# Token-major down and output projections, a new order in head and tail, and the mask of the maxima on DVE

## The reference

```python
xn = layernorm(x)                                   # over the 256 features, no weights
q, k, v = xn @ Wq.T, xn @ Wk.T, xn @ Wv.T           # 16 heads of 16
att = q @ k.T / 4 + causal_mask                     # 512 x 512 for each head
s = (softmax(att) @ v) @ Wo.T
g = silu( down( silu(gate(xn)) * up(xn) ) )         # 704 hidden; integer weights minus 128, times a scale per output row
out = x + s * g
```

## Time and profile before

| | us |
|---|---|
| median of 3 runs | 343.92 (342.92 to 345.23) |
| the profiled execution | 342.69 |
| its span | 340.7 |
| PE, DVE, ACT, POOL busy in the span | 304.8, 215.6, 168.8, 112.4 |

### The profile page before, as it was taken

How to read it: one execution, slowest core, us unless ns; L and a number is a source line. 1 busy time by engine, 2 the same in 40 slices (tenths; PEclk the granted TensorE clock), 3 DMA queues, 4 the chain that set the end, 5 groups by cost and what they waited for, 6 DMA issues and landing times.

```text
span 340.7 us, 5720 instructions
## 1 busy us (share of the span) xinstructions
PE 304.8 (89%) x2192; PEld 197.6 (58%) x2192; DVE 215.6 (63%) x364; ACT 168.8 (50%) x238; POOL 112.4 (33%) x179
## 2 busy tenths in 40 slices
PE   0695779999999989999999989999999999998855
PEld 0573447666565546766655547767656566664323
DVE  5799755644579986454769986554765666447113
ACT  3544325634475647343375646443475665336720
POOL 4014434311364552100355462100346662012310
PEclk9997879999999999999999999999999999999987
DMA  7846772078840003296750010187680100001201
GB/s 281 241 155 172 191 116 62 9 180 169 197 75 0 4 9 117 68 191 175 162 92 2 1 64 0 52 187 182 156 111 0 36 32 4 0 4 62 65 0 62
DMA packets 21150, 31.40 MB, mean 92 GB/s; under 512 B 2420, under 2 KB 10100, under 8 KB 21124
## 3 DMA queue, kind: packets, MB, share of 16 engines
q1 hardware_dynamic: 20672, 30.37, 37.5%
q10 hardware_dynamic: 452, 0.67, 0.6%
HBM read 20.19 MB, written 10.49 MB: 90 GB/s over the span
## 4 chain that ended last, share of the span: by engine, by line
PE 68%; DVE 19%; DMA 4%; ACT 4%; issue 3%; SPq 1%; POOL 0%; POOLq 0%; DVEq 0%; ACTq 0%
PE ps L349 14%; PE ps L351 12%; PE ps L350 11%; PE ps L518 10%; PE ps L499 7%; PE ps L458 6%; PE ps L470 4%; DVE mx L934 3%; DVE mx L932 3%; ACT hid L662 2%; DVE xn L900 2%; PE ps L526 2%; DVE hid L919 2%; DMA qk_scratch<-xr 2%; DVE nw L893 1%
## 5 line engine op out<-in xcount | busy, mean ns | idle before, releaser
L725 ACT ACTIVATE pt<-ps 128x1024 f32<-128x1024 f32 x80 | 81.8, 1023 | 24.5 <-PE ps L499 24.4
L839 POOL TENSOR_SCALAR_AFFINE_SELECT pt<-pt 128x256 f32<-128x256 f32 (+1 forms) x112 | 48.1, 442 | 128.7 <-ACT pt L725 128.7
L932 DVE TENSOR_REDUCE mx<-ps 128x2 f32<-128x1024 f32 x32 | 38.9, 1221 | 11.8 <-PE ps L470 11.1
L458 PE MATMUL ps<-kp,qp 48*128 48x512 f32 (+3 forms) x256 | 37.0, 347 | 9.3 <-DMA kp<-qk_scratch 3.5
L825 POOL TENSOR_TENSOR hl<-hid,hh 128x512 fp32r<-128x512 f32 x24 | 31.2, 1301 | 42.3 <-ACT hh L676 41.9
L819 POOL TENSOR_TENSOR hid<-hid 128x512 f32<-128x512 f32 x24 | 30.7, 1278 | 42.5 <-ACT hid L669 42.3
L518 PE MATMUL ps<-pt,vt 128*17 128x256 f32 (+3 forms) x512 | 43.8, 437 | 0.8 <-POOL pt L839 0.8
L349 PE MATMUL ps<-xh,guh 128*128 128x512 f32 x96 | 43.3, 451 | 0.0
L499 PE MATMUL ps<-qp,kp 50*128 50x512 f32 (+3 forms) x256 | 40.1, 370 | 2.9 <-DVE mx L935 1.6
L351 PE MATMUL ps<-xh,gul 128*128 128x512 f32 x96 | 38.7, 403 | 0.0
L350 PE MATMUL ps<-xl,guh 128*128 128x512 f32 x96 | 38.6, 402 | 0.0
(11 more groups left out here) (104 smaller groups left out, 495.1 us busy)
## 6 DMA issues: line engine op xcount, KB each, us to landing
qk_scratch<-hid SPq DMA_DIRECT2D x24, 256.0 KB
qp<-qk_scratch SPq DMA_DIRECT2D x14, 256.0 KB, 4.8
kp<-qk_scratch SPq DMA_DIRECT2D x14, 256.0 KB, 6.8
qp<-qk_scratch SPq DMA_DIRECT2D x18, 128.0 KB, 5.2
kp<-qk_scratch SPq DMA_DIRECT2D x18, 128.0 KB, 7.1
xr<-in_x SPq DMA_DIRECT2D x4, 512.0 KB, 4.1
out<-xr SPq DMA_DIRECT2D x8, 256.0 KB, 2.3
xin<-in_x SPq DMA_DIRECT2D x3, 512.0 KB, 3.7
```

Source lines behind the costliest of these rows:

```text
L458: nc.tensor.matmul(ps[:, base + e, c:c + w], qp[part, place(b, half), col, i * P:(i + 1) * P], kp[part, place(b, half), col, 0:w], start=( ...
L725: nc.scalar.activation(pt[:, 2 * kk:2 * kk + 2, :], ps[:, base:base + 2, :], ACT.Exp, scale=SCALE).then_inc(exp_done, 1)
L839: mm = nc.gpsimd.affine_select(out=diag, in_=diag, compare_op=ALU.is_ge, fill=0.0, base=0, pattern=[[0, diag.shape[1]], [1, P]], channel_m ...
L932: mm = nc.vector.tensor_reduce(mg[:, :, kk, 3], both, AX.X, ALU.max, negate=True)
```

## The change

- The causal mask of the maxima is added by DVE, to the diagonal blocks in PSUM, in all pairs from the ninth on (72 of 80); the first eight keep their mask matmuls. DVE waits for its own add before the reduction. POOL makes the mask tile `tri`.
- `down` and the output projection have the tokens on the partitions: stationary is the activation (128 x 128), moving the weight with 256 columns. "dn" and "o" have twice as many matmuls of half the columns.
- The transposes "y" and "yd" go. The scale `s_down` is multiplied into w_down by POOL in the head, and the factor 0.5 into Wo by ACT and DVE; the small DMAs of `sdt` go, one of `sdb` (128 copies of the 256 scales) comes. ACT's first copy of w_down waits for POOL.
- The residual additions go to POOL (units "r", steps 7 and 8 and the tail), but for the last one.
- The last batch's "oa" is finished at once: DVE multiplies it with u, POOL adds it to x. The last z2 is cut in two halves, in two banks.
- DVE's normalisation of batches 2 and 3 goes to ACT, in the same steps, with a shift that DVE makes once (`shifts`).
- In the head the maxima of pair 5 and the unit gu 8 come ahead of the first "c".

```diff
-    7: [("zt", 0, 0), ("c", 0, 2), ("dn", 0, 1)],
-    8: [("pv", 0, 3), ("y", -1, 0), ("y", -1, 1), ("gu", 1, 0)],
+    7: [("zt", 0, 0), ("c", 0, 2), ("dn", 0, 1), ("r", -1, 0)],
+    8: [("pv", 0, 3), ("r", -1, 1), ("gu", 1, 0)],
...
-TAIL = [..., ("z2", 0, 1), ("o", 0, 0), ("o", 0, 1), ("yd", 0, 0), ("yd", 0, 1)]
+TAIL = [..., ("z2", 0, 1), ("o", 0, 0), ("r", 0, 0), ("o", 0, 1), ("r", 0, 1)]
...
-           ("c", 0, 0), ("gu", 0, 8), ("m", 0, 5), ("m", 0, 6), ("gu", 0, 9), ("m", 0, 7)])
+           ("m", 0, 5), ("gu", 0, 8), ("c", 0, 0), ("m", 0, 6), ("gu", 0, 9), ("m", 0, 7)])
...
@@ sync
-            for k in range(KD):
-                sp.dma_start(sdt[:, k:k + 1], sd[k * P:(k + 1) * P].rearrange("(p o) -> p o", o=1)).then_inc(sc_loaded, 16)
...
+            sp.dma_start(sdb[:], sd.partition_broadcast(P)).then_inc(wd_loaded, 16)
...
@@ tensor, down
-                for m in range(HT):
-                    mm = split3(ps[:, bank, :], wdh[:, m, cols], wdl[:, m, cols], hh[:, m, :], hl[:, m, :],
-                                m == 0, m == HT - 1)
+                for i in (2 * n, 2 * n + 1):
+                    rows = slice(i * P, (i + 1) * P)
+                    for m in range(HT):
+                        mm = split3(ps[:, bank, (i % 2) * D:(i % 2 + 1) * D], hh[:, m, rows], hl[:, m, rows],
+                                    wdh[:, m, :], wdl[:, m, :], m == 0, m == HT - 1)
...
@@ tensor, maxima
-                for r in range(2):
+                for r in range(2 if n < LEAD else 0):
...
@@ scalar
+            def normalise(b, i):
+                if i == 0:
+                    act_e.wait_ge(shf_done, b - 1)
+                    act_e.wait_ge(xt_ready, KD * b)
+                nc.scalar.activation(xn[:, i, :], xin[:, i, :], ACT.Identity, scale=nw[:, 1, i:i + 1],
+                                     bias=shf[:, i:i + 1]).then_inc(xn_done, 1)
...
+                    if b + 2 < B and s >= 16:
+                        normalise(b + 2, s - 16)
...
@@ gpsimd
+            pool.wait_ge(wd_loaded, 32)
+            nc.gpsimd.tensor_scalar(raw_d, raw_d.bitcast(I32), -ZERO_POINT, None, ALU.add).then_inc(wd_shifted, 1)
+            pool.wait_ge(wd_shifted, 1)
+            raw_d3 = raw_d.rearrange("p (m n) -> p m n", m=HT)
+            nc.gpsimd.tensor_tensor(raw_d3, raw_d3, sdb[:].rearrange("p (o n) -> p o n", o=1).to_broadcast([P, HT, D]),
+                                    ALU.mult).then_inc(wd_scaled, 1)
...
+            def residual(b, n):
...
+                nc.gpsimd.tensor_tensor(part, u[:, b % 2, n, :], part, ALU.add).then_inc(out_done, 1)
...
@@ vector, maxima
+                if STEPS * b + m >= LEAD:
+                    if kk < 2:
+                        diag = both[:, :, 3 * P:]
+                        mask = tri[:].rearrange("p (o n) -> p o n", o=1).to_broadcast([P, 2, P])
...
+                    nc.vector.tensor_tensor(diag, diag, mask, ALU.add).then_inc(tri_added, 1)
+                    dve.wait_ge(tri_added, STEPS * b + m - LEAD + 1)
...
@@ vector, finish
-                nc.vector.scalar_tensor_tensor(ud, ps[:, BANK["o", b, d], :], hsd[:, d:d + 1], ud,
-                                               ALU.mult, ALU.mult).then_inc(fin_done, 1)
+                nc.vector.tensor_tensor(un, ps[:, BANK["o", b, n], :], un, ALU.mult).then_inc(fin_done, 1)
```

More of the change, by code:

```diff
@@ L532, in transpose_back, with project_out_part, project_out @@
                 for i in range(TT):
-                    mm = nc.tensor.transpose(ps[:, bank, i * P:(i + 1) * P], zn[:, i, half * P:(half + 1) * P], ident[:])
+                    at = bank + (i // 2 if (b, half) == (B - 1, 1) else 0)
+                    mm = nc.tensor.transpose(ps[:, at, i * P:(i + 1) * P], zn[:, i, half * P:(half + 1) * P], ident[:])
+                    if i == 1 and (b, half) == (B - 1, 1):
+                        mm.then_inc(z2_ready, 1)
                 mm.then_inc(z2_ready, 1)
-            def project_out(b, d):
-                bank = take(("o", b, d))
-                if d == 0:
+            def project_out_part(b, n, k, bank):
+                for i in (2 * n, 2 * n + 1):
+                    rows = slice(i * P, (i + 1) * P)
+                    mm = split3(ps[:, bank, (i % 2) * D:(i % 2 + 1) * D], zh[:, k, rows], zl[:, k, rows],
+                                woh[:, k, :], wol[:, k, :], True, True)
+                return mm
+            def project_out(b, n):
+                if b == B - 1:
+                    pe.wait_ge(zlo_done, 2 * b + 2 + n)
+                    project_out_part(b, n, 1, BANK["o", b, n]).then_inc(o_ready, 1)
+                    return
+                bank = take(("o", b, n))
+                if n == 0:
                     pe.wait_ge(zlo_done, 2 * (b + 1))
@@ L681, in ffn_tanh @@
                     act_e.wait_ge(u_done, KD * b + d)
-                if b == 0 and d == 0:
-                    act_e.wait_ge(sc_step, 3)
-                nc.scalar.activation(fth[:], ps[:, BANK["dn", b, d], :], ACT.Tanh, scale=hsd[:, d:d + 1]
-                                     ).then_inc(fth_done, 1)
+                nc.scalar.activation(fth[:], ps[:, BANK["dn", b, d], :], ACT.Tanh, scale=0.5).then_inc(fth_done, 1)
             def copy_c(b, g):
@@ L847, in unit @@
                     hidden_lo(b, n // 2 - 1)
+                elif kind == "r":
+                    residual(b, n)
+                elif kind == "oa":
+                    residual_first(b, n)
             for kind, b, n in HEAD_MIX:
@@ L857, in _ @@
                         unit(kind, of, n)
+            for kind, of, n in tail_units():
+                unit(kind, of, n)
         @block.vector
@@ new lines, in finish_first @@
+            def finish_first(b, n):
+                dve.wait_ge(oa_ready, n + 1)
+                nc.vector.tensor_tensor(u[:, (b + 1) % 2, n, :], ps[:, BANK["oa", b, n], :], u[:, b % 2, n, :],
+                                        ALU.mult).then_inc(fin_first, 1)
+            def residual(b, n):
+                if (b, n) != (B - 1, 1):
+                    return
+                dve.wait_ge(fin_done, KD * b + n + 1)
+                dve.wait_ge(out_first, 2)
+                part = xr[:, 2 * n:2 * n + 2, :].rearrange("p i d -> p (i d)")
+                nc.vector.tensor_tensor(part, u[:, b % 2, n, :], part, ALU.add).then_inc(last_out_done, 1)
```

180 lines of the change are left out of this document (95 added, 85 removed).

## The result

The changed kernel takes 351.45 us (median; 349.13 to 353.43 in four runs) against 343.42 us of the kernel before in runs beside it (342.81 to 345.23): a ratio of 1.022, 95% interval 1.017 to 1.027. I had forecast 344.6 with a range of 334 to 350. The profiled execution took 349.13 us with a span of 347.4, the fastest of the four; the medians are 8.0 us apart, the profiled spans 6.6.

A forecast was written before the change was run, and what follows sets the result against it. PE was taken as the bound, with DVE close behind in short steps. Terms -8.3 - 2.7 + 2.5 + 12.3 + 0.3 - 1.0 - 2.4 = +0.7 us on the median before, 343.92, gave 344.6 us, range 334 to 350.

The forecast's parts named there:

- Part 2: DVE adds the mask, 0.47 or 0.73 us each: PE's waits +12.3 us, ACT's normalisations +0.3.
- Part 1: Mask matmuls of the maxima leave PE: -0.14 us in 44 pairs, -0.075 in 28, sum -8.3 us, the low end.
- The high end: All of the mask's time leaves PE, 0.33 us a pair, 0.22 for the short mask: -20.7 us.
- rival A: In the main loop DVE stays hidden behind PE: faster, 335 us, with 329 as its end; chance 0.31.
- rival C: DVE's PSUM to PSUM add costs double, 1.2 us each: waits grow by +11, 355 us; chance 0.05.
- my list: Changes of PE's waits behind DVE's adds, by batch and step of the main loop: together +12.3 us.
- ACT's wait for DVE's shift: ACT's first normalisation waits for DVE's shift, with the exp of the next pair behind it: +0.3 us.
- Part 3: Token-major projections: "dn" and "o" cost +2.5 us, transposing y back goes, -2.7 us.
- Part 4: Head: scores start at 50 instead of 51.46, -1.5 us; ACT's w_down copy and gates slip behind POOL, +0.5.
- Part 5: Tail: last transposes go, last z2 halved, output half stored early, -2.7 us; POOL's early residuals +0.3.
- B: Head: DVE's gate scales stall behind POOL's w_down product, PE stands still: +4, 348.6 us; chance 0.17.
- D: The ACT normalisation or the reorder does nothing: +3 us at most, inside the range; no chance of its own.

The follow-up runs named there:

- e1: The changed kernel with the mask of the maxima back as matmuls on PE in all 80 pairs: 342.26 us, ratio 0.996 to the kernel before.
- e2: The changed kernel with the mask of the maxima left out from the ninth pair on (computation incomplete): 330.86 us, ratio 0.961 to the kernel before.
- e10: The changed kernel with a step's first unit ahead of its maxima, only in chosen steps of batches 0 to 2: median 353.0 us, no ratio.
- e4: The kernel before with only the mask of the maxima moved to DVE from the ninth pair on: 360.16 us, ratio 1.044.
- e6: The changed kernel with POOL's, ACT's and DVE's w_down work later and ACT's first c copy earlier: 349.68 us, ratio 1.020 to the kernel before.
- e9: The changed kernel with DVE adding the mask in 32 pairs of long steps, PE elsewhere, ACT's normalisations one step later: 336.25 us, ratio 0.982 to the kernel before.

## Why the prediction was wrong

The frame held: steps that PE bounds became shorter without the mask, and steps in which PE waits for DVE became longer with the add. The sum did not. By spans, my +0.7 was -5.3 for all but the mask (the steps 17 and 19 of "Part 2" counted with it), -8.3 for PE's mask and +14.3 for the add. The runs show -1.0, -11.5 and +19.1, which is +6.6. Of the 4.3 us missing in the first, 1.4 are the head and 0.5 the tail; 1.5 are steps 0 and 1 of batch 0, which ran at a lowered clock in e1, and 0.9 ACT's normalisation. The step that failed most is the price of the add's waits: PE stood still about as long as forecast, but its matmuls also ran slower, which I had put at nothing.

**Part 1, the mask leaves PE: mis-sized, -8.3 for -11.5.** The reading that failed is that of the gap without a mask from a score row before the z2 transposes (315.70 to 316.13 in the earlier trace rows). The gap depends on the unit that follows: 0.33 to a "gu" unit, 0.43 to a pv unit. So 0.24 went and not 0.14, and 0.13 and not 0.075 for the short mask. The high end (all of the 0.33) was wrong as well. And a gap under 0.35 was what I had set down as a sign of rival A: it came, but only before "gu" units.

**Part 2, the adds: right in duration and in the time that PE stands still; the slower matmuls behind were missing.** The adds took 427 and 695 ns, just the rows, and rival C is out:

```profile
L992 DVE TENSOR_TENSOR ps<-ps,tri 128x512 f32<-128x512 f32 x44 | 30.6, 695 | 9.2 <-PE ps L462 9.0
...
L992 DVE TENSOR_TENSOR ps<-ps,tri 128x256 f32<-128x256 f32 x28 | 12.0, 427 | 9.4 <-PE ps L462 9.2
```

Step 10 of batch 2 grew by 0.75 (forecast 0.7), and batch 2 lost 2.8 us (after less e2), against some 2.9 in my list; I had one of its waits in a wrong place (step 1, not step 0). The sum over the others failed: batch 0 lost 6.7 instead of 3.4, batch 1 4.8 instead of 4.0, batch 3 5.4 instead of 3.9. (Head and tail took 0.5 off.) Here are batches 0 and 3 as whole windows, in the changed kernel and (second fence) in e2, which has the same matmuls:

```profile
50.92:130.05 79.13, 71.00 (x464) 47.35 (x465) 59.53 (x102) 41.28 (x62) 28.29 (x42) 0.96 0.34 75
280.96:332.95 51.99, 45.14 (x387) 29.93 (x387) 31.21 (x52) 26.18 (x34) 17.76 (x33) 0.97 0.07 22
```

```profile
52.05:124.44 72.39, 67.62 (x466) 45.60 (x466) 48.58 (x83) 40.97 (x62) 28.39 (x42) 1.00 0.39 82
267.80:314.41 46.61, 43.61 (x387) 29.42 (x388) 24.45 (x40) 26.10 (x34) 17.82 (x33) 1.00 0.08 25
```

Length less busy time of PE is what it stands still: 3.4 us more than in e2 in batch 0 and 3.9 in batch 3, and in the same way 3.9 in batch 1 and 2.1 in batch 2. That is 13.2 together, for the 14.3 of my list. The rest is the same matmuls taking longer: 3.4 us in batch 0 and 1.5 in batch 3, at clocks of 0.96 and 0.97 for 1.00, and 1.6 in the two batches at full clock (why those grew is open; the ends of matmuls are modelled). The lowered clock can be seen in three steps: step 14 of batch 0 took 1.25 us more than the same step of batch 1; in step 10 of batch 0 PE is busy 4.85 us for what takes 3.51 in batches 1 and 2; in step 10 of batch 3 2.69 for 1.91 or so (step 0's and e2's figure). Together 3.4 us. In all three PE had just stood still (1.40 us for the reduction in step 14, 1.75 for the c rows ahead of step 10, 1.79 for the reduction in step 10 of batch 3). I had priced a wait at its own length and at nothing for the slower matmuls behind it. That these waits brought the clock down is argued from their place, and not every wait does: in e10 PE waited 2.56 us for the c rows at the end of the same step 9 of batch 0, and step 10 then ran at full clock (3.45 us). No run separates the two.

**Part 2, ACT's wait for DVE's shift: mis-sized, 0.15 a batch (+0.3 for two) for 1.1.** Step 17 took 4.28 instead of 3.13 in e1 as in the changed kernel, in both batches. In the timeline DVE's shift (1.09 us) ends only at 200.87, ACT's first normalisation starts at 200.90, and the exp that PE's next scores need is queued behind it. With steps 18, 19 and 0 counted (-0.6, +0.4, -1.36) the part brings 0.4 a batch; I had 0.85. e4 suggests that together with the adds it brings more.

**Part 3, projections: right.** In e1 step 7 of batch 1 (a "dn") grew by 0.21 and step 8, which lost the transposes, fell from 4.24 to 3.42, near the forecast. Only an "o" was cheaper than my 0.14: steps 5 and 6 grew by 0.07 and 0.05.

**Part 4, head: the gain of 1.0 was not there.** The scores started 0.5 us earlier in the changed kernel and 0.4 and 0.6 later in e1 and e2, and between 50.7 and 53.0 over all the kernels with this same head, so that one trace can't tell a gain of 1.0. What held up first was DVE: with w_down's low part (2.22 us, from 33.77) ahead of the first two reductions PE waited 4.23 us for them, to 37.18. I had given that slip 0.5. The reductions' delay went on to the c rows: ACT issued them at 47.46, 3.3 us later than before, where I had 0.4. The bound behind it, the landing of the c rows, was right, as e6 shows.

**Part 5, tail: -1.9 for -2.4.** The transposes are gone; the size was 0.5 too large, and no run looked into it.

**The rivals.** A (DVE hidden) had one half right: PE gained more than the low end. But where DVE bounds the step nothing could hide the add. B's mechanism took place and cost PE 2.70 us, but nothing on the first maxima: they started at 30.31 (30.76 before), and at 30.73 in e6, which has no such hole but waits 3.0 us for their transfer. D is part of the result. **The range** ended at 350; two of the three sums were off upward, by 4.3 and 4.8, and the third gave back only 3.2. The scatter helped to miss it: the profiled execution, 349.13 us, lies inside the range, and the median is 2.3 us above it.

## What to carry to other kernels

An add that moves from the bounding engine to the next one is worth its time only in the steps where that engine has room: price both lengths per step, and move it in those alone (e9, with 32 of the 72 adds and the normalisation a step later, is 1.8% faster than before; the change, with all 72, is 2.2% slower). A new wait of PE should be priced with the matmuls behind it at the lower clock as the other end of its range: here 13.2 us of standing still came with 6.5 of longer matmuls. And before PE's order is changed to fill a wait, count what the order itself costs: here 0.14 to 0.38 us in each step that had the new one, which I put down to changes of matrix shape.

## What was unexpected of the hardware

- A POOL conversion of 1536 elements a partition from int32 to float took 4.29 us (4.53 in e6), and held a DVE instruction with one input and six elements for 3.46 us instead of 0.16.
- The time from the start of four maxima matmuls without a mask to the next unit depends on that unit: 0.33 us to a 512-column matmul, 0.43 to a pv unit.
- Runs of one and the same kernel differ, and with them the clock they are granted: the changed kernel's four runs are 349.13 us at a mean clock of 0.966, 349.89 at 0.953, 353.02 at 0.949 and 353.43 at 0.944. The changed kernel scatters over 4.3 us in these four, the kernel before over 2.4 in the four beside them, but over 6.6 in the thirteen runs beside e1 to e4.
- The c rows, 8 KB a transfer, took up to 6.6 us from the start of their issue to their landing in e6, where the repacking transfers were under way.
